# State-space convolution and FFN on one core: constants in another form and partly on GpSimd, another order around the first and last block

## The chip, the core and the metric

One core of one Trainium2 chip. The metric is the time of one execution in microseconds (us), for which before and after are compared by the median of several runs. The engines are TensorE (PE; PEld is its loading of weights), VectorE (DVE), ScalarE (ACT), GpSimd (POOL) and SyncE (SP, which here only issues DMAs).

## The reference

```python
# x: (128, 32, 512) f32, length: (128,)
K = 2 * Re(sum_n Ct[h,n] * exp(dtA[h,n] * l))            # (32, 512), Ct = C (exp(dtA) - 1) / A
y = causal_conv(x, K, over l) + x * D                     # channel by channel
y = y * (l < length[b])
x_q = fp8(y / in_scale); gate, up = x_q @ Wg.T, x_q @ Wu.T   # 512 -> 1376
hidden = silu(gate) * up
out = x + fp8(hidden / in_scale) @ Wd.T                   # 1376 -> 512
```

A is complex, with a real part -exp(log_A_real) and an imaginary part A_imag, and dtA = A dt. Rounding to fp8 is done in f32 arithmetic (a sum with a magnitude, a difference, a clip), the matmuls in bf16.

## The kernel before

The 32 channels are done in 8 blocks of 4, each with 4 x 128 = 512 tokens. A channel's convolution is one product of a Toeplitz matrix, cut from K with its D added at lag 0, with the transposed x: four f32 matmuls of 512, 384, 128 and 256 columns (L489). A block then has 11 chunks of the hidden width (c = 0 to 10, `slots`). For each, PE makes gate and up (L547, 4 + 4 matmuls of 512 columns), ACT the silu (L398), DVE the product `hv` (L860). Two chunks make a pair e = 0 to 5. For each pair ACT takes the magnitude `hc` (L381), DVE adds (`ht`, L868), rounds (`hq`, L877) and clips (L885), and `hq` is the operand of the down matmuls (L503), which PE does one block later, 4 a chunk. A convolution's result is masked (L825), scaled and rounded in the same way (L362 to L373 on ACT; `yt` L833, `yq` L844, L851 on DVE), one block ahead; the convolutions run up to two blocks ahead (CONV_PLAN).

The order is written out by hand on every engine. The tables at the end of the file (MASK_PLAN, SUM_PLAN, ROUND_PLAN, H_BEHIND, H_EVEN, H_LAST, OUT_SLOTS) say in which chunk a step of DVE or ACT stands. Chunk c of gate and up writes bank c mod 2 (with the block's parity) and so waits for the product of chunk c - 2 (L537). Pairs 3, 4 and 5 of a block are finished in the next one (`left_over`). The last block has no convolutions, and its own down matmuls stand behind it (L588 to L601), with the residual added by DVE (L892) and stored in five parts (LAST_PARTS).

Ahead of the blocks K has to be made. The parameters come in, DVE computes dt and A dt (to L686), from there exp(dtA) - 1 and C times it over A (L712 to L776), and with cos, sin and exp of the steps (`waves`, `decayed`) the operands `gk` of K (`g_of`, L788 to L792). This goes in three groups of channels: 4, 8 and 20 (K_GROUPS counts pairs). PE multiplies (`k_of`, L450, L454), the rows are copied out of PSUM (L802), SP stores them in DRAM (L241) and reads them back as Toeplitz matrices (L248, L252). Between, PE runs matmuls whose results are not used (`warm`, L471 and L459; WARM says how many). GpSimd issues the weight loads: `wg` and `wu`, the first 256 columns at once (L288, L289), the rest after the Toeplitz matrices.

## Time and profile before

| | us |
|---|---|
| median of 3 runs (325.57 to 326.49) | 325.71 |
| the profiled execution's own time | 325.52 |
| its span, first to last instruction | 323.8 |
| PE busy in it | 310.2 |
| DVE busy | 303.2 |
| ACT busy | 206.9 |

1.7 us of the profiled execution's time lie outside the span. The rows read below are from three views: the timeline (instructions of an engine in order of time, equal ones merged with their count), the waits, and the DMA issues. "x4" of an f32 matmul is two instructions, as each leaves two records; some records are missing ("x3" for four). A matmul's end is modelled: four of 512 columns are given as 1.03 us, while the next one starts 0.86 us after the first of them.

### The profile page before, as it was taken

How to read it: one execution, taken by the hardware profiler on the slowest of the kernel's cores; microseconds unless marked ns; L12 is line 12 of the kernel's file. 1: busy time of each engine (PE TensorE's matmuls, PEld its weight loads, DVE VectorE, ACT ScalarE, POOL GpSimd, SP SyncE). 2: the span in 40 equal slices, each digit the busy share in tenths (PEclk: the TensorE clock that was granted, in tenths of full speed). 3: DMA queues.
4: the chain of work that ended last, by engine and by line, in shares of the span. 5: the costliest groups of instructions: out<-in, count | busy, mean ns of one | idle time of the engine just before them, and what ended most of it. 6: DMA issues, size and time to landing. Idle time of an engine off the chain costs nothing.

```text
span 323.8 us, 4771 instructions
## 1 busy us (share of the span) xinstructions
PE 310.2 (96%) x1569; PEld 162.9 (50%) x1595; DVE 303.2 (94%) x464; ACT 206.9 (64%) x318; POOL 12.5 (4%) x20
## 2 busy tenths in 40 slices
PE   1999999999999999999999999999999999989996
PEld 1467554545455554555455454555455454534444
DVE  6999999999999999999998999989998999989784
ACT  4858788188755777486845868376863959364540
POOL 2031000000001000010001000010001000010010
PEclk9999999999999999999999999999999999999999
DMA  6879999300002690078202780067401650051028
GB/s 201 181 181 231 268 278 383 148 1 2 0 0 28 150 343 3 1 130 279 110 0 36 165 317 1 0 121 249 150 0 16 134 243 0 0 97 34 2 31 228
DMA packets 14014, 38.38 MB, mean 119 GB/s; under 512 B 1470, under 2 KB 6558, under 8 KB 11052
## 3 DMA queue, kind: packets, MB, share of 16 engines
q1 hardware_dynamic: 8412, 26.58, 23.2%
q0 software_dynamic: 5584, 11.57, 20.6%
q8 instruction: 10, 0.16, 0.2%
q14 instruction: 8, 0.07, 0.1%
HBM read 33.90 MB, written 15.81 MB: 154 GB/s over the span
## 4 chain that ended last, share of the span: by engine, by line
PE 72%; DVE 19%; issue 4%; ACT 4%; DMA 1%; DVEq 0%; ACTq 0%
PE gate_ps L547 19%; PE up_ps L547 18%; PE down_ps L503 17%; PE y_ps L489 15%; DVE hv L860 3%; DVE yq L844 3%; DVE yt L833 2%; DVE hq L877 2%; DVE ht L868 2%; PE y_ps L598 1%; DVE ym L825 1%; PE down_ps L598 1%; ACT hc L381 1%; DMA prm<-in_params 1%; DVE hq L885 1%
## 5 line engine op out<-in xcount | busy, mean ns | idle before, releaser
L398 ACT ACTIVATE sil<-gate_ps,fac 128x512 f32<-128x512 f32 (+1 forms) x88 | 59.6, 680 | 67.8 <-PE gate_ps L547 66.8
L547 PE MATMUL gate_ps<-yq,wg 128*128 128x512 bf16 (+3 forms) x365 | 88.2, 363 | 2.7 <-DVE hv L860 2.4
L547 PE MATMUL up_ps<-yq,wu 128*128 128x512 bf16 (+3 forms) x367 | 88.4, 363 | 0.3
L489 PE MATMUL y_ps<-xt,toep 128*128 128x512 f32 (+1 forms) x248 | 78.1, 434 | 0.0
L503 PE MATMUL down_ps<-wd,hq 128*128 128x512 bf16 (+1 forms) x295 | 76.8, 379 | 0.7
L860 DVE SCALAR_TENSOR_TENSOR hv<-up_ps,fac,sil 128x512 f32<-128x512 f32 (+1 forms) x88 | 65.5, 744 | 8.2 <-ACT sil L398 6.6
L381 ACT ACTIVATE hc<-hv 128x1024 f32<-128x1024 f32 (+1 forms) x48 | 47.0, 980 | 20.9 <-DVE hq L877 19.8
L547 PEld LDWEIGHTS gate_ps<-yq,wg 128*128 128x128 bf16 x372 | 35.6, 100 | 43.6 <-ACT sil L398 4.0
L489 PEld LDWEIGHTS y_ps<-xt,toep 128*128 128x128 f32 x248 | 45.9, 190 | 19.9 <-issue 2.4
L868 DVE SCALAR_TENSOR_TENSOR ht<-hc,hv 128x1024 f32<-128x1024 f32 (+1 forms) x48 | 54.1, 1127 | 1.9 <-ACT hc L381 1.9
L547 PEld LDWEIGHTS up_ps<-yq,wu 128*128 128x128 bf16 x372 | 36.3, 100 | 38.3
L877 DVE SCALAR_TENSOR_TENSOR hq<-hc,ht 128x1024 bf16<-128x1024 f32 (+1 forms) x48 | 53.8, 1126 | 0.3
L503 PEld LDWEIGHTS down_ps<-wd,hq 128*128 128x128 bf16 (+1 forms) x308 | 30.1, 98 | 37.9 <-issue 12.6
L844 DVE SCALAR_TENSOR_TENSOR yq<-yc,yt 128x1024 bf16<-128x1024 f32 x32 | 39.0, 1217 | 0.1
L833 DVE SCALAR_TENSOR_TENSOR yt<-yc,yv 128x1024 f32<-128x1024 f32 x31 | 37.7, 1217 | 0.0
L370 ACT ACTIVATE yc<-ym,fac 128x512 f32<-128x512 f32 x32 | 22.8, 713 | 2.9 <-DVE yq L844 2.9
L362 ACT ACTIVATE yv<-ym,fac 128x512 f32<-128x512 f32 x31 | 22.1, 712 | 3.2 <-DVE ym L825 3.2
L373 ACT ACTIVATE yc<-ym,fac 128x512 f32<-128x512 f32 x32 | 22.8, 712 | 0.0
L363 ACT ACTIVATE yv<-ym,fac 128x512 f32<-128x512 f32 x31 | 22.0, 709 | 0.0
L825 DVE TENSOR_TENSOR ym<-y_ps,mask 128x512 f32<-128x512 f32 x31 | 21.1, 681 | 0.0
L388 ACT ACTIVATE res<-down_ps,fac 128x512 f32<-128x512 f32 x28 | 19.0, 679 | 2.2 <-PE down_ps L503 2.1
L885 DVE TENSOR_SCALAR hq<-hq 128x1024 bf16<-128x1024 bf16 (+1 forms) x48 | 18.4, 397 | 0.3
(155 smaller groups left out, 118.1 us busy)
## 6 DMA issues: line engine op xcount, KB each, us to landing
xt<-in_xT SPq DMA_DIRECT2D x8, 1024.0 KB, 7.6
out<-in_x SPq DMA_DIRECT2D x7, 1024.0 KB, 5.6
out<-res POOLq DMA_DIRECT2D x7, 1024.0 KB, 7.8
toep<-kpad_scratch SPq DMA_DIRECT2D x6, 1024.0 KB, 10.0
toep<-kpad_scratch SPq DMA_DIRECT2D x8, 256.0 KB, 3.9
wd<-in_down POOLq DMA_DIRECT2D x1, 1280.0 KB, 21.3
xt<-in_x SPq DMA_DIRECT2D x1, 1024.0 KB, 7.3
out<-xt SPq DMA_DIRECT2D x3, 256.0 KB, 3.1
```

Source lines behind the costliest of these rows:

```text
L370: gate = nc.scalar.activation(yc[q][:, 0, :], ym[q][:], ACT.Abs, scale=fac[:, R_GATE:R_GATE + 1])
L381: nc.scalar.activation(hc[e % 2][0:w, 0:k], hv[e % 2][0:w, 0:k], ACT.Abs, scale=UP20).then_inc(abs_ready, 1)
L398: nc.scalar.activation(sil[b][0:w, :], gate_ps[b][0:w, :], ACT.Silu, scale=fac[0:w, S_GATE:S_GATE + 1]).then_inc(silu_done, 1)
L489: last = nc.tensor.matmul(y_ps[h % 2][:, d * P:L], toep[par][:, h, d * P:(d + 1) * P], xt[par][:, h, 0:L - d * P], start=(d == 0), stop=(d ...
L503: mm = nc.tensor.matmul(down_ps[t % 2][:], hq[par][0:w, k, t * P:(t + 1) * P], wd[0:w, k, :], start=(k == 0), stop=(k == CH - 1))
L547: mm = nc.tensor.matmul(ps[b][0:w, cols], wt[:, k, c * P:c * P + w], yq[par][:, version, k, cols], start=(k == 0), stop=(k == LB - 1))
L825: v.tensor_tensor(ym[q][:], y_ps[q][:], mask[:].rearrange("p k b -> p (k b)"), ALU.mult).then_inc(ym_done, 1)
L833: v.scalar_tensor_tensor(yt[q][:], yc[q][:], FLOOR, yv[q][:], ALU.max, ALU.add).then_inc(yt_done, 1)
L844: v.scalar_tensor_tensor(yq_of(par, h), yc[q][:].rearrange("p v (k b) -> p (v k) b", k=LB), FLOOR, yt[q][:].rearrange("p v (k b) -> p (v k ...
L860: v.scalar_tensor_tensor(hv[c // 2 % 2][0:w, c % 2], up_ps[b][0:w, :], fac[0:w, S_UP:S_UP + 1], sil[b][0:w, :], ALU.mult, ALU.mult).then_i ...
L868: v.scalar_tensor_tensor(ht[e % 2][0:w, 0:k], hc[e % 2][0:w, 0:k], FLOOR, hv[e % 2][0:w, 0:k], ALU.max, ALU.add).then_inc(t_done, 1)
L877: v.scalar_tensor_tensor(hq[par][0:w, 2 * e:2 * e + k, :], hc[e % 2][0:w, 0:k], FLOOR, ht[e % 2][0:w, 0:k], ALU.max, ALU.subtract, reverse ...
```

## The change

It has five parts. (1) The constants. With E = exp(Re dtA) - 1, h = 2 C / A and Q = h (exp(i Im dtA) - 1), the coefficient 2 Ct is (E + 1) Q + E h. The square of A's magnitude and the numerator of h come from five small products, sums and differences on GpSimd (L299 to L305 of the new file), behind a wait for `decay_ready` and ahead of its wait for the Toeplitz matrices. The D term of the first group is put into its bank ahead of time (`unit_terms(0)`, an operand 64 columns wider in `in_unit`). The lengths' masks move behind work for the second group. (2) WARM: one f32 matmul of 213 columns ahead of `k_of(0)` and one behind, 8 of 512 columns ahead of `k_of(1)` and 2 behind, for 2 and 14. (3) `hv` has three buffers. (4) Order: the fourth `yt` sum of each block is in chunk 9 for 8. At the boundaries 0 to 1 and 6 to 7 (SUM_BEHIND) the clip of pair 2 and the magnitude and sum of pair 4 come behind the first product of the next block; in block 7 the rest is spread over one chunk more. ACT's loop over blocks 1 to 4 is written out. (5) In block 7 the down matmuls of block 6 use four banks (`y_ps` as well) and another order, 4, 8, 6, 6, 5, 4, 4, 3, 2, 2 and 0 a chunk for 4 each; the last part of the output is 128 columns for 256.

```diff
-WARM = (2, 14)
+WARM = (1, 1, 8, 2)
...
-        hv = [sb(f"hv{i}", [P, 2, TOK]) for i in range(2)]
+        hv = [sb(f"hv{i}", [P, 2, TOK]) for i in range(3)]
...
+        unit_tile = inside(hq[0], JC * M, 1, P + FIRST * KB)
+        one_by_one = unit_tile[:, :, 0:P]
+        dsk_first = unit_tile[:, 0, P:].rearrange("p (j b) -> p j b", b=KB)
...
+            pool.wait_ge(decay_ready, 1)
+            nc.gpsimd.tensor_tensor(s(27), s(9), s(9), ALU.mult).then_inc(gain_chain, 1)
+            nc.gpsimd.tensor_tensor(s(31, 2), s(37, 2), s(9).broadcast_to([P, 2, JC]), ALU.mult).then_inc(gain_chain, 1)
+            pool.wait_ge(gain_chain, 1)
+            nc.gpsimd.tensor_tensor(s(27), s(27), s(28), ALU.add).then_inc(norm_ready, 1)
+            pool.wait_ge(gain_chain, 2)
+            nc.gpsimd.tensor_tensor(s(33), s(31), s(30), ALU.subtract)
+            nc.gpsimd.tensor_tensor(s(34), s(29), s(32), ALU.add).then_inc(gain_ready, 1)
...
-                nc.scalar.activation(hc[e % 2][0:w, 0:k], hv[e % 2][0:w, 0:k], ACT.Abs, scale=UP20).then_inc(abs_ready, 1)
+                nc.scalar.activation(hc[e % 2][0:w, 0:k], hv[e % 3][0:w, 0:k], ACT.Abs, scale=UP20).then_inc(abs_ready, 1)
...
+                from_bank = y_ps[t % 2] if isinstance(g, int) and g == NBLK - 2 and t >= 2 else down_ps[t % 2]
+                nc.scalar.activation(res[par][:, t, :], from_bank[:], ACT.Copy,
...
+                    if c == 0 and g - 1 in SUM_BEHIND:
+                        abs_prod(PAIRS * g - 2, PAIRS - 2, n - 1)
+                    if c and c % 2 == 0 and not (c == CH - 1 and g in SUM_BEHIND):
...
-            with act.Fori(0, (NBLK - 4) // 2) as j:
+            for j in range((NBLK - 4) // 2):
...
+                    if i == 0:
+                        nc.tensor.matmul(k_in_bank(0, half), unit_row, dsk_first[row], start=True, stop=False)
+                    else:
+                        nc.tensor.matmul(k_in_bank(i, half)[:, :, 0], unit_row, dsk[row, js],
+                                         start=False, stop=True).then_inc(k_ready, 1)
...
-                            nc.tensor.matmul(k_in_bank(i, half)[:, j - js.start], gk[rows, j, t],
-                                             wave[rows, j, t, 0:KB], start=(j == js.start and t == 0), stop=False)
-                for half in range(2):
-                    row = slice(N * half, N * half + 1)
-                    nc.tensor.matmul(k_in_bank(i, half)[:, :, 0], cst[row, UNIT:UNIT + KA], dsk[row, js],
-                                     start=False, stop=True).then_inc(k_ready, 1)
+                            last = i == 0 and j == js.stop - 1 and t == 1
+                            mm = nc.tensor.matmul(k_in_bank(i, half)[:, j - js.start], gk[rows, j, t],
+                                                  wave[rows, j, t, 0:KB], start=(i > 0 and j == js.start and t == 0),
+                                                  stop=last)
+                            if last:
+                                mm.then_inc(k_ready, 1)
+                if i:
+                    unit_terms(i)
...
-            for n in range(WARM[0]):
-                nc.tensor.matmul(y_ps[n % 2][:, 0:6 * JC + CONSTS], prm[:, 0:P], prm[:], start=True, stop=True)
+            unit_terms(0)
+            warm_small(WARM[0])
             k_of(0)
+            warm_small(WARM[1])
             pe.wait_ge(gate_in, 16)
-            warm(WARM[1])
+            warm(WARM[2])
             k_of(1)
+            warm(WARM[3])
...
+            def wide_down_part(g, par, c):
+
+                lo = sum(WIDE_COUNTS[:c])
+                for t, k in WIDE_ORDER[lo:lo + WIDE_COUNTS[c]]:
+                    w = width(k)
+                    if t == 0:
+                        pe.wait_ge(hq_ready, PAIRS * g + k // 2 + 1)
+                    if k == 0 and t < 2:
+                        pe.wait_ge(out_done, EMPTY + HB * g + t - 1)
+                    if k == 0 and t >= 2:
+                        pe.wait_ge(ym_done, HB * NBLK)
+                    mm = nc.tensor.matmul((y_ps if t >= 2 else down_ps)[t % 2][:], hq[par][0:w, k, t * P:(t + 1) * P],
+                                          wd[0:w, k, :], start=(k == 0), stop=(k == CH - 1))
+                    if k == CH - 1:
+                        mm.then_inc(down_ready, 1)
...
+                if down and not ahead:
+                    wide_down_part(g - 1, 1 - par, c)
+                elif down:
...
-                                    (2, range(6, CH), full), (3, range(CH), slice(0, L // 2)),
-                                    (3, range(CH), slice(L // 2, L))):
+                                    (2, range(6, CH), full), (3, range(CH), slice(0, 3 * P)),
+                                    (3, range(CH), slice(3 * P, L))):
...
-                    if t >= 2 and k == 0:
-                        pe.wait_ge(out_done, EMPTY + HB * (NBLK - 1) + t - 3)
+                    if k == 0:
+                        pe.wait_ge(out_done, EMPTY + HB * (NBLK - 2) + t + 1)
...
-            c = did(v.scalar_tensor_tensor(norm, ar, 0.5, ar, ALU.mult, ALU.mult))
+            v.tensor_scalar(two_x.bitcast(I32), kx, 127.0, 2.0 ** 23, ALU.add, ALU.mult)
+            dve.wait_ge(norm_ready, 1)
+            c = did(v.reciprocal(norm, norm))
             after(b)
             b = did(v.scalar_tensor_tensor(qx, qx, 1.0 / math.factorial(4), rx, ALU.add, ALU.mult))
-            v.tensor_tensor(c_ar, cc, both(ar), ALU.mult)
             after(b)
             b = did(v.scalar_tensor_tensor(qx, qx, 1.0 / math.factorial(3), rx, ALU.add, ALU.mult))
-            c = did(v.tensor_tensor(norm, norm, half, ALU.add))
+            v.tensor_tensor(rt_x, rx, two_x, ALU.mult)
+            dve.wait_ge(gain_ready, 1)
+            after(c)
+            c = did(v.tensor_tensor(h, h, both(norm), ALU.mult))
             after(b)
             b = did(v.scalar_tensor_tensor(qx, qx, 1.0 / math.factorial(2), rx, ALU.add, ALU.mult))
-            v.tensor_scalar(two_x.bitcast(I32), kx, 127.0, 2.0 ** 23, ALU.add, ALU.mult)
-            after(b)
-            b = did(v.scalar_tensor_tensor(qx, qx, 1.0, rx, ALU.add, ALU.mult))
-            c = did(v.reciprocal(norm, norm))
-            after(b)
-            b = did(v.tensor_tensor(qx, qx, two_x, ALU.mult))
-            v.tensor_tensor(gre, s(30), s(31), ALU.subtract)
-            c = did(v.tensor_tensor(gim, s(29), s(32), ALU.add))
+            dve.wait_ge(sines_ready, 1)
+            a = did(v.scalar_tensor_tensor(cos1, s(SIN_HALF), -2.0, s(SIN_HALF), ALU.mult, ALU.mult))
+            after(b)
+            b = did(v.scalar_tensor_tensor(qx, qx, 1.0, rt_x, ALU.add, ALU.mult))
             after(c)
+            c = did(v.tensor_tensor(h_sin, h, both(s(SIN)), ALU.mult))
+            after(a)
+            a = did(v.tensor_tensor(h_cos, h, both(cos1), ALU.mult))
+            after(b)
             b = did(v.scalar_tensor_tensor(expm1, two_x, -1.0, qx, ALU.add, ALU.add))
-            dve.wait_ge(sines_ready, 1)
-            a = did(v.scalar_tensor_tensor(sr, s(SIN_HALF), -2.0, s(SIN_HALF), ALU.mult, ALU.mult))
-            c = did(v.tensor_tensor(g, g, both(norm), ALU.mult))
             after(a)
-            a = did(v.scalar_tensor_tensor(sr, expm1, 1.0, sr, ALU.add, ALU.mult))
-            b = did(v.scalar_tensor_tensor(si, expm1, 1.0, s(SIN), ALU.add, ALU.mult))
+            v.tensor_tensor(s(35), s(29), s(32), ALU.subtract)
+            a = did(v.tensor_tensor(s(36), s(31), s(30), ALU.add))
             damped = [decayed(0)]
+            after(b)
             after(a)
-            a = did(v.tensor_tensor(sr, sr, expm1, ALU.add))
-            after(b)
-            b = did(v.tensor_tensor(g_si, g, both(si), ALU.mult))
+            v.scalar_tensor_tensor(h_cos, both(expm1), 1.0, turned, ALU.add, ALU.mult)
+            a = did(v.tensor_tensor(h_sin, both(expm1), h, ALU.mult))
             after(a)
-            a = did(v.tensor_tensor(g_sr, g, both(sr), ALU.mult))
-            after(a)
-            v.tensor_tensor(s(38), s(29), s(32), ALU.add)
-            a = did(v.tensor_tensor(s(39), s(31), s(30), ALU.subtract))
+            a = did(v.tensor_tensor(s(38, 2), h_cos, h_sin, ALU.add))
...
-            after(last)
-            v.tensor_scalar(mask[:, 0, :], lenf[:], cst[:, LEN0:LEN0 + 1], None, ALU.is_gt)
             after(w)
             v.tensor_tensor(turns[:, js], turns[:, js], whole[:, js], ALU.subtract).then_inc(turns_ready, 1)
             js = K_GROUPS[2]
             w = did(v.tensor_tensor(in_steps(turns[:, js]), tau_by_j(js), steps(js), ALU.mult))
+            after(last)
+            v.tensor_scalar(mask[:, 0, :], lenf[:], cst[:, LEN0:LEN0 + 1], None, ALU.is_gt)
+            after(w)
+            w = did(v.tensor_scalar(whole[:, js], turns[:, js], MAGIC, MAGIC, ALU.add, ALU.subtract))
             v.tensor_scalar(mask[:, 1, :], lenf[:], cst[:, LEN0 + 1:LEN0 + 2], None, ALU.is_gt)
             after(w)
-            w = did(v.tensor_scalar(whole[:, js], turns[:, js], MAGIC, MAGIC, ALU.add, ALU.subtract))
+            v.tensor_tensor(turns[:, js], turns[:, js], whole[:, js], ALU.subtract).then_inc(turns_ready, 1)
+            damped.append(decayed(1))
+            g_of(1)
             v.tensor_scalar(mask[:, 2, :], lenf[:], cst[:, LEN0 + 2:LEN0 + 3], None, ALU.is_gt)
-            after(w)
-            v.tensor_tensor(turns[:, js], turns[:, js], whole[:, js], ALU.subtract).then_inc(turns_ready, 1)
             v.tensor_scalar(mask[:, 3, :], lenf[:], cst[:, LEN0 + 3:LEN0 + 4], None, ALU.is_gt).then_inc(scales_ready, 1)
-            g_of(1)
+            damped.append(decayed(2))
...
+                    at_least(dve, t_done, m - 2)
+                v.scalar_tensor_tensor(hv[c // 2 % 3][0:w, c % 2], up_ps[b][0:w, :], fac[0:w, S_UP:S_UP + 1],
...
-            def left_over(g, par, c, before):
+            def left_over(g, par, c, before, behind):
 
                 last = PAIRS * g - 1
                 if c == 0:
                     if PAIRS - 3 not in before.values():
                         rounded(last - 2, g - 1, 1 - par, PAIRS - 3)
-                    rounded(last - 1, g - 1, 1 - par, PAIRS - 2)
+                    if not behind:
+                        rounded(last - 1, g - 1, 1 - par, PAIRS - 2)
                 if c == 1:
                     clip(last - 2, 1 - par, PAIRS - 3)
+                    if behind:
+                        rounded(last - 1, g - 1, 1 - par, PAIRS - 2)
+                    else:
+                        clip(last - 1, 1 - par, PAIRS - 2)
+                    rounded_sum(last, PAIRS - 1)
+                    if not behind:
+                        rounded(last, g - 1, 1 - par, PAIRS - 1)
+                        clip(last, 1 - par, PAIRS - 1)
+                if c == 2 and behind:
                     clip(last - 1, 1 - par, PAIRS - 2)
-                    rounded_sum(last, PAIRS - 1)
                     rounded(last, g - 1, 1 - par, PAIRS - 1)
                     clip(last, 1 - par, PAIRS - 1)
...
+                    if c == 0 and g - 1 in SUM_BEHIND:
+                        clip(PAIRS * g - 4, 1 - par, PAIRS - 4)
+                        rounded_sum(PAIRS * g - 2, PAIRS - 2)
...
-                        if PAIRS - 3 not in plan.values():
-                            clip(PAIRS * g + PAIRS - 4, par, PAIRS - 4)
-                        rounded_sum(m - 1, PAIRS - 2)
+                        if g not in SUM_BEHIND:
+                            if PAIRS - 3 not in plan.values():
+                                clip(PAIRS * g + PAIRS - 4, par, PAIRS - 4)
+                            rounded_sum(m - 1, PAIRS - 2)
...
-SUM_PLAN = {2: 0, 3: 1, 6: 2, 8: 3}
...
+SUM_PLAN = {2: 0, 3: 1, 6: 2, 9: 3}
...
+SUM_BEHIND = (0, NBLK - 2)
...
+WIDE_ORDER = [(t, k) for chunks in (range(6), range(6, CH)) for t in range(HB) for k in chunks]
+WIDE_COUNTS = [4, 8, 6, 6, 5, 4, 4, 3, 2, 2, 0]
...
-              (HB - 1, 0, slice(0, L // 2)), (HB - 1, 1, slice(L // 2, L))]
+              (HB - 1, 0, slice(0, 3 * P)), (HB - 1, 1, slice(3 * P, L))]
```

The diff is cut to what the text speaks of; left out are the operand of the D term, the bank of each tile at the end (now `down_ps`, `down_ps`, `y_ps`, `y_ps`), and the products with -2 C at the start of DVE's chain, one instruction more.

The first place is VectorE while the constants of the kernel K are computed, from the turns of the first two channels to the copy of their K out of PSUM. `sm` holds all small operands. Before:

```order
L751 TENSOR_SCALAR sm<-sm 128x16
L753 SCALAR_TENSOR_TENSOR sm<-sm 128x16 [waits chain]
L754 RECIPROCAL sm<-sm 128x16
L756 TENSOR_TENSOR sm<-sm 128x16 [waits chain]
L757 TENSOR_TENSOR sm<-sm 128x16
L758 TENSOR_TENSOR sm<-sm 128x16
L760 SCALAR_TENSOR_TENSOR sm<-sm 128x16 [waits chain]
L762 SCALAR_TENSOR_TENSOR sm<-sm 128x16 [waits sines_ready]
```

The same place now, with two waits for GpSimd:

```order
L799 TENSOR_SCALAR sm<-sm 128x16
L801 RECIPROCAL sm<-sm 128x16 [waits norm_ready]
L803 SCALAR_TENSOR_TENSOR sm<-sm 128x16 [waits chain]
L805 SCALAR_TENSOR_TENSOR sm<-sm 128x16 [waits chain]
L806 TENSOR_TENSOR sm<-sm 128x16
L809 TENSOR_TENSOR sm<-sm 128x32 [waits chain,gain_ready]
L811 SCALAR_TENSOR_TENSOR sm<-sm 128x16 [waits chain]
L813 SCALAR_TENSOR_TENSOR sm<-sm 128x16 [waits sines_ready]
```

Between line 741 and the first product with `wave` (L788 before, L843 now) stood 24 instructions and stand 19 now. Five others are on GpSimd, between its early weight loads and the next. The row L299 ISA is an instruction that the builder puts ahead of the first arithmetic on this engine; its name in the built program is a reload of the engine's code library, index 0. GpSimd now:

```order
L293 DMA wu<-in_up 128x4x256
L299 ISA
L299 TENSOR_TENSOR sm<-sm 128x16 [waits decay_ready]
L300 TENSOR_TENSOR sm<-sm 128x32
L302 TENSOR_TENSOR sm<-sm 128x16 [waits gain_chain]
L304 TENSOR_TENSOR sm<-sm 128x16 [waits gain_chain]
L305 TENSOR_TENSOR sm<-sm 128x16
L307 DMA wg<-in_gate 128x4x384 [waits toep_first3]
```

Before, L289 was followed by L291 (now L307) directly.

The second place is VectorE at the boundary from block 6 to block 7 (`hv` is a product, `ht` the sum that rounds it, `hq` the rounded operand of the down matmuls). Before:

```order
L860 SCALAR_TENSOR_TENSOR hv<-up_ps,fac,sil 96x512 [waits t_done,up_ready,silu_done]
L877 SCALAR_TENSOR_TENSOR hq<-hc,ht 128x1024 [waits t_done]
L885 TENSOR_SCALAR hq<-hq 128x1024 [waits hr_done]
L868 SCALAR_TENSOR_TENSOR ht<-hc,hv 128x1024 [waits hr_done,abs_ready]
L860 SCALAR_TENSOR_TENSOR hv<-up_ps,fac,sil 128x512 [waits t_done,up_ready,silu_done]
L877 SCALAR_TENSOR_TENSOR hq<-hc,ht 128x1024 [waits t_done] x2
```

Now:

```order
L917 SCALAR_TENSOR_TENSOR hv<-up_ps,fac,sil 96x512 [waits t_done,up_ready,silu_done]
L934 SCALAR_TENSOR_TENSOR hq<-hc,ht 128x1024 [waits t_done]
L917 SCALAR_TENSOR_TENSOR hv<-up_ps,fac,sil 128x512 [waits t_done,up_ready,silu_done]
L942 TENSOR_SCALAR hq<-hq 128x1024 [waits hr_done]
L925 SCALAR_TENSOR_TENSOR ht<-hc,hv 128x1024 [waits hr_done,abs_ready]
L934 SCALAR_TENSOR_TENSOR hq<-hc,ht 128x1024 [waits t_done]
L917 SCALAR_TENSOR_TENSOR hv<-up_ps,fac,sil 128x512 [waits up_ready,silu_done]
```

The first product of block 7 now stands ahead of the clip and the sum that finish block 6, and the second ahead of one rounding more. The boundary from block 0 to 1 has the same exchange, with both roundings ahead of the second product.


## Rows read from the trace of the kernel before

**Rows 1.** The page, part 1: busy time and share of the span of each engine

```profile
PE 310.2 (96%) x1569; PEld 162.9 (50%) x1595; DVE 303.2 (94%) x464; ACT 206.9 (64%) x318; POOL 12.5 (4%) x20
```

**Rows 2.** Waits of PE: waited for, us in total, times, longest

```profile
PE gate_ps L547 <- DVE hv L860: 2.4, 5, 1.0
```

**Rows 3.** Timeline of PE before the first block: start us, us, instruction, [idle before]

```profile
12.40 4.57 PE L459 MATMUL y_ps<-wg 128*128 128x512 bf16 x14
16.90 0.64 PE L450 MATMUL gate_ps<-res,hq 64*16 64x32 f32 x32
17.77 0.92 PE L560 MATMUL y_ps<-xt,toep 128*128 128x256 f32 x4
```

**Rows 4.** Timeline of VectorE (DVE) in the same stretch

```profile
8.09 0.17 DVE L741 SCALAR_TENSOR_TENSOR sm<-sm 128x16 f32<-128x16 f32 x1
...
10.97 0.23 DVE L788 TENSOR_TENSOR hq<-res,sm 128x64 f32<-128x64 f32 x1
...
12.50 0.34 DVE L802 COPY hq<-down_ps 16x64 f32<-16x64 f32 x2 [0.27 <-PE down_ps L454]
12.78 0.27 DVE L804 TENSOR_SCALAR mask<-lenf,prm 128x128 f32<-128x128 f32 x1
```

**Rows 5.** DMA issues of SyncE, and the landing of those of line 248

```profile
12.87 0.36 SPq L241 DMA_DIRECT2D kpad_scratch<-hq  x1
14.36 1.75 SPq L248 DMA_DIRECT2D toep<-kpad_scratch  x4
```

```profile
DMA to landing us min/median/max: 3.4/3.7/4.0
```

**Rows 6.** Timeline of GpSimd (POOL) before the first block, then early DMAs to landing

```profile
0.88 0.19 POOL L284 MEMSET zrow<- 32x128 f32 x1 [0.29 <-POOLq L1072]
3.96 0.93 POOL L288 DMA_DIRECT2D wg<-in_gate  x1 [2.89 <-DMA kpad_scratch<-zrow]
4.88 0.77 POOL L289 DMA_DIRECT2D wu<-in_up  x1
```

```profile
wg<-in_gate POOLq DMA_DIRECT2D x1, 256.0 KB, 8.4
```

**Rows 7.** Timeline of ScalarE (ACT): a load of its function table

```profile
7.05 1.28 ACT L328 ACT_TABLE_LOAD   x1
```

**Rows 8.** Block 0 to block 1: PE, then DVE

```profile
61.43 0.82 PE L547 MATMUL gate_ps<-yq,wg 128*128 128x384 bf16 x4 [0.60 <-DVE hv L860]
```

```profile
60.45 0.74 DVE L860 SCALAR_TENSOR_TENSOR hv<-up_ps,fac,sil 128x512 f32<-128x512 f32 x1
...
65.09 0.41 DVE L885 TENSOR_SCALAR hq<-hq 128x1024 bf16<-128x1024 bf16 x1
65.76 1.23 DVE L868 SCALAR_TENSOR_TENSOR ht<-hc,hv 128x1024 f32<-128x1024 f32 x1 [0.26 <-ACT hc L381]
67.13 0.75 DVE L860 SCALAR_TENSOR_TENSOR hv<-up_ps,fac,sil 128x512 f32<-128x512 f32 x1
```

**Rows 9.** Block 6 to block 7: timeline of PE

```profile
285.15 1.03 PE L503 MATMUL down_ps<-wd,hq 128*128 128x512 bf16 x4
287.19 1.02 PE L547 MATMUL gate_ps<-yq,wg 128*128 128x512 bf16 x4 [1.01 <-DVE hv L860]
288.05 1.03 PE L547 MATMUL up_ps<-yq,wu 128*128 128x512 bf16 x4
...
297.40 1.26 PE L503 MATMUL down_ps<-wd,hq 128*128 128x512 bf16 x4
```

**Rows 10.** The end: PE, then DVE

```profile
309.73 1.03 PE L547 MATMUL up_ps<-yq,wu 128*96 128x512 bf16 x4
```

```profile
310.86 0.75 DVE L860 SCALAR_TENSOR_TENSOR hv<-up_ps,fac,sil 96x512 f32<-96x512 f32 x1 [0.69 <-ACT sil L398]
...
315.91 0.29 DVE L885 TENSOR_SCALAR hq<-hq 96x512 bf16<-96x512 bf16 x1
...
321.21 0.48 DVE L892 SCALAR_TENSOR_TENSOR xt<-gate_ps,fac,xt 128x256 f32<-128x256 f32 x1 [0.72 <-PE gate_ps L598]
```

53 lines of the change are left out of this document (31 added, 22 removed).

## The prediction

> **What bounds the kernel now.** I read the page first: PE is busy for 310.2 us of 323.8 and DVE for 303.2 [rows 1]. Two engines are nearly full, so a step is worth what the engine that is late at that place gains. Of PE's waits, those of gate matmuls for a product of DVE are 2.4 us in five places [rows 2]. The timeline puts them at 37.9 us (block 0 begins), at 61.4 (block 0 to 1) and at 287 to 293 (6 to 7). In between PE has no idle time, and blocks repeat every 37.15 us. The chunks around the first and the last blocks hold more DVE work than PE work, since PE has no down matmuls in block 0 and no or few convolutions in 6 and 7.
>
> Ahead of the blocks the end is set by a chain: constants on DVE (L741 at 8.09, operands at 10.97), rows of K, their copy at 12.50 [rows 4], their store at 12.87 and the Toeplitz loads at 14.36, of which the first lands 3.4 us later, at 17.7 [rows 5], and the first convolution at 17.77 [rows 3]. From there PE runs without a gap to 35. The matmuls of the warm-up (14 in 4.57 us from 12.40, where 14 at 0.216 would take 3.0) begin at 0.43 us each, the lower clock (1.2 GHz), and end at 0.216, the higher one (2.4 GHz) [rows 3]; in their starts the change lies at 15.3 us.
>
> **The chain to the first convolution.** Between 8.09 and 10.97, 24 instructions stand, 0.12 us each [rows 4]; five fewer give 0.6 us. One more at the start of DVE's chain costs 0.05. The two D matmuls of the first group, 0.14 us ahead of the copy at 12.50, go to before the constants are ready, where PE has a gap. So the copy comes at 11.8, 0.7 us earlier, the store at 12.2, and by the same 1.5 and 3.4 us the first Toeplitz matrix at 17.0. The store now meets the end of the early weight loads; the bound for that is 0.3 us of the 0.7.
>
> The second group must be through PE by then. DVE's operands for it were ready at 16.85 (PE began on them at 16.90 [rows 3]). They come 0.7 us earlier by the copy, and about 0.4 more since two masks (0.27 us long, pitch 0.2 [rows 4]) are now behind them: 15.8. PE, with one small warm-up (0.9 us) after the first group, starts the eight large ones at 12.6, six of them at 0.43 and the last at 0.216 if the clock rises where it did: 15.7. The second group takes 0.8, to 16.6, two further matmuls 0.43, to 17.05. The convolution starts at 17.1 to 17.3: I take **-0.6 us** (bounds -0.3 and -0.75). DVE's first mask, at 19.57 before, has the whole 0.7 us and doesn't hold this up.
>
> What GpSimd does has to be in time. It is free at 5.65 (4.88 + 0.77 [rows 6]), the norm is wanted at 8.26 and the gain at 8.72 (8.09 plus the pitches ahead). No row shows arithmetic on GpSimd. Its memset of 32x128 took 0.19 us [rows 6]; five of that are 0.95, from 6.1 to 7.05. The upper end is a DMA issue's 0.93 each, 4.65: gain at 10.7, 2.0 late. The nearest in kind is the memset, so 0. Ahead of them stands the reload of its code library, which no row shows either. Below, the nearest row is ACT's load of its function table, 1.28 us [rows 7]: 5.65 + 1.28 + 0.95 is 7.9, in time. Above it is a transfer in the same stretch: the 256 KB of `wg`, issued at 3.96, took 8.4 us to land [rows 6]. Up to 2.1 us are hidden. I take the table load, since it is the same kind of step, and keep the transfer as a rival.
>
> The Trainium skill (GPSIMD Engine Reference, section 4.1) puts two-input elementwise work on GpSimd at about half VectorE's speed. By DVE's 0.17 us for such tiles that would be 5 x 0.34, ready at 7.8 without the reload: the same conclusion as from the memset.
>
> **Block 0 to 1.** PE sat idle 0.60 us for the product of chunk 9 at 60.45 [rows 8]. With the `yt` sum (1.13 us of pitch) behind it, that product is at 59.3 and PE's gap goes. Next comes DVE's own gap: from the clip at 65.09 to the first product of block 1 at 67.13 there are 2.04 us for 0.34 + 1.14 of work, as DVE waits for ACT's magnitude (0.26) and then for the semaphore [rows 8]. The product is now first, silu is ready by 64.2, and the 0.56 us go. DVE has no further idle time until 84.7 us, where PE once more waits 0.2 us for a product, so PE gets what DVE gains: **-0.55 us** (bounds 0, and -0.9 with all that PE loses there).
>
> **Block 6 to 7.** Three waits for products, 1.01, 0.18 and 0.22, plus 0.16 each, because an end is modelled 0.16 us late (the matmuls at 285.15 are through at 286.02, the next start at 287.19 [rows 9]): 1.9 us. At 297.40 four down matmuls took 1.10 us to the next start instead of 0.86, waiting for ACT to empty a bank [rows 9]: 0.23. With four banks that goes. In the new order the first product of block 7 is at 284.0 (silu of the last part of chunk 0 ends then) instead of 286.29, the second at 287.4 instead of 289.2. PE, with 4 and 8 down matmuls in chunks 0 and 1, asks for them at 286.9 and 289.9. Going on like this to chunk 10, I find each product at least 1 us early. The clip of pair 2 ends as PE comes to its matmuls (both 285.1), 0 to 0.1 us. So PE gains 2.1 us and ends the last up matmul at 309.36 instead of 311.46.
>
> Some of it is given back. Before, the last up matmuls ended at 310.59, DVE took the product at 310.86 and had the last clip at 316.20, 5.34 us later [rows 10]; PE wanted it at 316.65. Now no down matmul stands behind the last up matmuls: product at 309.63, last clip at 314.97, wanted 24 matmuls after 309.36, at 314.55. With 0.05 for the semaphore that is a new wait of 0.5. Sum **-1.6 us** (bounds -0.9 and -2.1).
>
> **The tail.** Both halves of the last tile stay at 11 x 512 columns together. The last residual of 256 columns took 0.48 us [rows 10]; for 128 it is about 0.13 less, and its store is smaller: **-0.1** (0 to -0.2). The third `hv` buffer takes away waits that show none of PE's idle time: 0 by itself, but it lets products go ahead of sums. ACT's written-out loop: 0, it is idle 1 to 3 us in each block.
>
> **Sum.** -0.6 - 0.55 - 1.6 - 0.1 = -2.85 against the profiled execution's 325.52: 322.67. The median is 0.19 above that execution, so 322.8. By the bounds alone: 321.7 to 324.5. A measurement of this kernel can tell about 0.3% (1 us) from no change.
>
> **Rivals.** (a) *The reload costs what a transfer costs.* With 8.4 us it ends at 14.05, the gain is ready at 15.0, and DVE, which waits for it in order at 8.72, has everything behind it 6.3 us later: the rows of K, all masks, the first convolution. PE idles from 10.5 on. The blocks' gains stay, so the time is 322.8 + 6.3 = 329.1; if PE then starts its convolutions at the lower clock, up to 1.5 more. The reload decides from 2.1 us on, and at 5.0 us (2.1 + 2.9) the change is worth nothing. For it: code has to come from somewhere, and DMA is full from 5 us on. Against: ACT's load of the same sort is 1.28 us beside the same traffic.
>
> (b) *The two engines hold each other up.* Five GpSimd instructions of 0.19 us that each stop DVE once give 0.95 us: 323.7. The Trainium skill (SBUF, section on who interferes with whom) says that a VectorE instruction with two SBUF inputs and a GpSimd one that reads SBUF lock each other out; most of DVE's instructions between 6.1 and 8.7 are such, and no row here has both at work.
>
> (c) *The clock is not up when the convolutions start.* PE has less work before 15.3 us than before. Eight warm-ups at 0.43 end at 16.0, two at 0.43 end at 17.9 with the group, and the first channel takes 4.4 us for 2.2: 322.8 + 0.6 + 2.2 = 325.6, no change.
>
> **How the numbers follow.** Forecast 0.50, (a) 0.36, (b) 0.07, (c) 0.07. The likeliest case gives 322.8, its own range 321.7 to 324.5. The range reaches from 321.9 to 330.6 to hold most of (a) too. Faster is the forecast, (b) and some of (c): 0.58. Same: the rest of (c) and a reload of about 5 us, 0.06. Slower: 0.36.
>
> **What would show it.** In the new profile: GpSimd's first arithmetic at about 7 us, DVE's reciprocal (L801) without idle time before it, operands of K at 10.4, the copy at 11.8, the first convolution at 17.2; no idle time of PE at 61 and 287, and one of 0.4 us before the last down matmuls of tile 0. Wrong: GpSimd's products at 13 us or later with DVE idle until then (a); DVE instructions of 16 columns that take 0.3 (b); 512-column matmuls of 0.43 us after 16 us (c). If PE still idles at 287, my order of products is wrong.

## The result and the profile after

Over 7 runs each, the changed kernel takes 323.43 us (323.10 to 324.86) and the one before 325.82 (325.57 to 326.76): a ratio of 0.9933, with a 95% interval of 0.992 to 0.9945. That is 2.4 us less in this comparison; over the later comparisons the kernel before stays at 325.6 and the difference is 2.1.

The changed kernel has two profiles. The first, of its slowest run (324.86 us, span 323.2), has one disturbed stretch, told below. The second is of the same kernel (the first experiment, 323.38 us, span 321.7) and is typical; rows are of this one unless the text says otherwise. The table puts them beside [rows 3, 8, 9, 10].

| start, us | before | after, 2nd profile | after, 1st profile |
|---|---|---|---|
| first convolution | 17.77 | 17.63 | 19.14 |
| gate matmuls of chunk 7, block 1 | 84.70 | 84.17 | 85.64 |
| gate matmuls of block 7 | 280.81 | 280.29 | 281.77 |
| first of the last down matmuls | 311.46 | 308.94 | 310.42 |
| span | 323.8 | 321.7 | 323.2 |

GpSimd, as the timeline of the first profile has it (start us, us, instruction), answers to [rows 6]:

```profile
5.04 0.76 POOL L293 DMA_DIRECT2D wu<-in_up  x1
6.09 0.21 POOL L299 TENSOR_TENSOR sm<-sm 128x16 f32<-128x16 f32 x1 [0.29 <-DVE sm L743]
6.27 0.25 POOL L300 TENSOR_TENSOR sm<-sm 128x32 f32<-128x32 f32 x1
...
6.86 0.26 POOL L305 TENSOR_TENSOR sm<-sm 128x16 f32<-128x16 f32 x1
```

The five operations take 0.21 to 0.26 us each, 0.2 apart, and are through at 7.12; no reload of a library is seen ahead of them. Nor is one hidden behind the wait for VectorE: in the profile of the run with both mended (the last but two below) GpSimd's last early DMA issue ends at 6.03 and its first operation starts at 6.12, without idle time. By the Trainium skill (GPSIMD Engine Reference, section 4.1), at half VectorE's speed, the estimate was 0.34 each and 7.8; they are quicker than that.

VectorE in the second profile [rows 4]:

```profile
8.12 0.17 DVE L798 SCALAR_TENSOR_TENSOR sm<-sm 128x16 f32<-128x16 f32 x1
8.20 0.17 DVE L799 TENSOR_SCALAR sm<-sm 128x16 int32<-128x16 f32 x1
8.28 0.25 DVE L801 RECIPROCAL sm<-sm 128x16 f32<-128x16 f32 x1
...
10.48 0.22 DVE L843 TENSOR_TENSOR hq<-res,sm 128x64 f32<-128x64 f32 x1
...
11.87 0.34 DVE L857 COPY hq<-down_ps 16x64 f32<-16x64 f32 x2
```

VectorE waits for nothing at L801. The step that began at 8.09 before begins at 8.12, K's operands come 0.49 us earlier and the copy 0.63 earlier. PE and SyncE [rows 3, 5]:

```profile
12.64 3.56 PE L496 MATMUL y_ps<-wg 128*128 128x512 bf16 x8
16.13 0.64 PE L482 MATMUL gate_ps<-res,hq 64*16 64x32 f32 x32
...
16.84 0.61 PE L496 MATMUL y_ps<-wg 128*128 128x512 bf16 x2
17.63 0.92 PE L617 MATMUL y_ps<-xt,toep 128*128 128x256 f32 x4 [0.18 <-DMA toep<-kpad_scratch]
```

```profile
12.24 0.36 SPq L245 DMA_DIRECT2D kpad_scratch<-hq  x1
14.18 1.75 SPq L252 DMA_DIRECT2D toep<-kpad_scratch  x4
```

The store leaves 0.63 us earlier than before, but the Toeplitz loads that wait for it leave only 0.18 earlier: it takes 1.94 us now and took 1.49 before. PE is ready for the convolution and waits for the load.

In the first profile the same store and loads stand at 12.22 and 14.34, but the loads landed after 4.8 us at the soonest, where before they took 3.4 [rows 5]. A table by stretches (width, busy times by engine, PEclk, DMA share, GB/s) shows the DMA engines occupied and moving next to nothing:

```profile
15.00:15.50 0.50, 0.26 (x2) 0.00 (x0) 0.47 (x3) 0.50 (x2) 0.00 (x0) 1.00 0.99 29
15.50:16.00 0.50, 0.18 (x12) 0.18 (x14) 0.50 (x4) 0.50 (x1) 0.00 (x0) 1.00 1.03 29
```

No other profile here has it. From the first convolution on the two profiles of the changed kernel keep 1.5 us apart to the end.

### The profile page after: what moved, and what is told of

Same layout as the page of the kernel before. It is cut to its first block, busy times and chain, and to the rows that moved or that the text cites. A ratio compares the mean times of both kernels' runs of the same rounds, so it can differ in the third digit from the quotient of the medians.

```text
span 323.2 us, 4716 instructions
## 1 busy us (share of the span) xinstructions
PE 310.3 (96%) x1591; PEld 161.8 (50%) x1591; DVE 303.1 (94%) x460; ACT 206.5 (64%) x318; POOL 13.7 (4%) x25
## 4 chain that ended last, share of the span: by engine, by line
PE 77%; DVE 15%; issue 3%; DMA 3%; ACT 2%; DVEq 0%; SPq 0%
PE gate_ps L604 20%; PE up_ps L604 20%; PE down_ps L542 17%; PE y_ps L528 15%; DVE hv L917 3%; DVE yq L901 2%; DVE ht L925 2%; DVE yt L890 2%; DVE hq L934 2%; PE down_ps L558 2%; PE y_ps L558 1%; DMA toep<-kpad_scratch 1%; DVE ym L882 1%; PE y_ps L655 1%; DMA kpad_scratch<-hq 1%
## 5 line engine op out<-in xcount | busy, mean ns | idle before, releaser
L604 PE MATMUL gate_ps<-yq,wg 128*128 128x512 bf16 (+2 forms) x372 | 89.5, 363 | 0.5 <-DVE hv L917 0.3
L604 PE MATMUL up_ps<-yq,wu 128*128 128x512 bf16 (+2 forms) x372 | 89.5, 363 | 0.0
L542 PE MATMUL down_ps<-wd,hq 128*128 128x512 bf16 (+1 forms) x264 | 67.9, 379 | 0.0
L397 ACT ACTIVATE hc<-hv 128x1024 f32<-128x1024 f32 (+1 forms) x48 | 47.0, 980 | 17.1 <-DVE hq L934 16.7
L542 PEld LDWEIGHTS down_ps<-wd,hq 128*128 128x128 bf16 (+1 forms) x264 | 25.8, 98 | 32.7 <-issue 12.0
L942 DVE TENSOR_SCALAR hq<-hq 128x1024 bf16<-128x1024 bf16 (+1 forms) x48 | 18.5, 396 | 0.3
L405 ACT ACTIVATE res<-down_ps,fac 128x512 f32<-128x512 f32 x26 | 17.6, 677 | 1.0 <-PE down_ps L542 1.0
```

Of the source, the lines that this page charges most:

```text
L397: nc.scalar.activation(hc[e % 2][0:w, 0:k], hv[e % 3][0:w, 0:k], ACT.Abs, scale=UP20).then_inc(abs_ready, 1)
L542: mm = nc.tensor.matmul(down_ps[t % 2][:], hq[par][0:w, k, t * P:(t + 1) * P], wd[0:w, k, :], start=(k == 0), stop=(k == CH - 1))
L604: mm = nc.tensor.matmul(ps[b][0:w, cols], wt[:, k, c * P:c * P + w], yq[par][:, version, k, cols], start=(k == 0), stop=(k == LB - 1))
```

## Experiments

Times are medians; before is 325.6 us in all three comparisons (325.63, 325.58 and 325.67). Each kernel's median is over 5 to 12 runs. A ratio in brackets is to the kernel before, followed by its 95% interval.

**The changed kernel again.**

> The changed kernel once more, unaltered. My sum (prologue -0.6, block 0 to 1 -0.5, block 7 -1.6, tail -0.1) put it at 322.8 us; its median was 323.4, and in the one profile of it the transfers of K came in 1.4 to 2 us later than before. If that lateness was chance, this profile has the first convolution at 17.1 to 17.5 us and the Toeplitz loads landing 3.4 to 4.0 us after issue. If it belongs to the change (the earlier store meets the end of the weight loads every time), the convolution starts at 18.5 to 19.1 again and the loads take 4.8 us or more. Median 323.1 to 323.8 in either case.

Measured: 323.53 us (0.9932, interval 0.9918 to 0.9946). The convolution is at 17.63 and the four loads take 3.4 to 4.1 us, 3.8 in the middle: neither the 17.1 to 17.5 of the one theory nor the 18.5 of the other. The slow loads of the first profile were chance (one of 14 profiles has them, and their cause stays open); the slow *store* is not, as the next runs show.

**The start alone, and the blocks alone.** The first part of the change on the kernel before, and parts two to five on it.

> The kernel before with the first part of the change alone (complex product, five operations on GpSimd, D matmuls first, warm-ups 1, 1, 8, 2), the blocks as before. By my sum -0.6 us (325.2). By the rival that the transfers of K eat the earlier store: 0, between -0.2 and +0.2, or later than before where the loads take 4.8 us, up to +1.3.

> The kernel before with the rest of the change (third product buffer, order at blocks 0 to 1 and 6 to 7, four banks, last part of 128 columns), the start as before. By my sum -2.25 us (323.5 to 323.6), PE without idle time at 61 and 287, a wait of 0.5 ahead of the last down matmuls of tile 0. If the prologue gives nothing, this one has the time of the whole change (323.4). If the blocks had brought less than I put down and the prologue its 0.6, it would be at 324.0.

Measured: the start alone 325.41 us (0.999, 0.998 to 1.0), the blocks alone 323.75 (0.9941, 0.9927 to 0.9954). That is 0.22 and 1.88 us less, 2.10 together, which is the whole change. The start alone can't be told from nothing by its time; by its profile the convolution begins at 17.56 after a store of 2.0 us (issued at 12.31, loads at 14.30). With the blocks alone the start is row for row as before: convolution at 17.77, store 1.48 us.

The profile of the blocks alone prices each place in a clean way. Block 0 to 1, two rows of PE before that [rows 8] does not have, then PE and DVE with the blocks alone:

```profile
71.55 1.02 PE L547 MATMUL gate_ps<-yq,wg 128*128 128x512 bf16 x4
...
280.81 0.82 PE L547 MATMUL gate_ps<-yq,wg 128*128 128x384 bf16 x4
```

```profile
60.72 0.81 PE L568 MATMUL gate_ps<-yq,wg 128*128 128x384 bf16 x4
...
71.14 1.02 PE L568 MATMUL gate_ps<-yq,wg 128*128 128x512 bf16 x4 [0.26 <-DVE hv L881]
```

```profile
59.36 0.74 DVE L881 SCALAR_TENSOR_TENSOR hv<-up_ps,fac,sil 128x512 f32<-128x512 f32 x1
60.02 1.22 DVE L854 SCALAR_TENSOR_TENSOR yt<-yc,yv 128x1024 f32<-128x1024 f32 x1
61.27 1.23 DVE L865 SCALAR_TENSOR_TENSOR yq<-yc,yt 128x1024 bf16<-128x1024 f32 x1
...
65.26 0.73 DVE L881 SCALAR_TENSOR_TENSOR hv<-up_ps,fac,sil 128x512 f32<-128x512 f32 x1
```

PE's wait at 61 is gone (61.43 to 60.72) and half of it comes back at 71, where PE waits for DVE: 71.55 to 71.14, and at block 7 280.81 to 280.46. So this place gives 0.35 us (0.40 if counted from the first gate matmuls of 512 columns, which were at 37.98 for 37.93 already). DVE closed its gap of 0.56 but lost 0.11 on the way: its `yt` sum and the rounding that reads it now stand side by side, and the second begins 1.25 us after the first, where two independent ones of this size are 1.14 apart. The other 0.05 up to the 0.40 that its products gain (70.66 to 70.26) it was late before: its sum at 57.84 is at 57.89 here.

Block 7 [rows 9, 10], first the row of before at which its own last down matmuls begin:

```profile
311.46 3.62 PE L598 MATMUL y_ps<-wd,hq 128*128 128x512 bf16 x16
```

```profile
280.46 0.81 PE L568 MATMUL gate_ps<-yq,wg 128*128 128x384 bf16 x4
...
284.91 1.90 PE L522 MATMUL down_ps<-wd,hq 128*128 128x512 bf16 x8
286.65 1.03 PE L568 MATMUL gate_ps<-yq,wg 128*128 128x512 bf16 x4
...
309.12 3.62 PE L619 MATMUL down_ps<-wd,hq 128*128 128x512 bf16 x16
...
313.87 0.60 PE L619 MATMUL down_ps<-wd,hq 128*128 128x512 bf16 x2
314.77 1.04 PE L619 MATMUL down_ps<-wd,hq 96*128 96x512 bf16 x4 [0.31 <-DVE hq L906]
```

No wait for a product is left at 285 to 300; one of 0.11 for the clip of pair 2 stands ahead of the down matmuls at 284.91 (the up matmuls from 283.94 are through at 284.80). The last up matmuls are through at 309.12 instead of 311.46, of which 0.35 came with block 1: block 7 gives 1.99. The new wait for the last clip is there: two down matmuls of 0.216 are followed after 0.90, so 0.47.

**GpSimd's five operations back on VectorE.** Between the same steps of the two chains, for example:

```diff
-            dve.wait_ge(norm_ready, 1)
+            d = did(v.tensor_tensor(s(34), s(29), s(32), ALU.add))
+            after(c)
             c = did(v.reciprocal(norm, norm))
```

> The whole change, but the five operations of GpSimd put back on VectorE between the same steps of the two chains, where none waits for its forerunner. By my price of 0.12 us each the operands of K, their copy and the first convolution come 0.6 us later, and the time is up by 0.6, if K's transfers take the same. If the transfers absorb what the start gains (they end when the early weight loads are through), the time is up by 0 to 0.2, and the Toeplitz loads land at the same time as in the change.

Measured: 323.69 us (0.9936, 0.9923 to 0.9948), 0.16 more than the change, which is within the spread of the single runs. The copy is at 12.28 (0.41 later than 11.87) and the store at 12.65; this transfer takes 1.76, so the loads leave at 14.41 and the convolution starts at 17.79. Of 0.41 us in the chain 0.16 reach the convolution: K's transfers absorb the rest, most of it in the store (1.76 for 1.94), as the second theory says; that they end when the early weight loads are through is not shown by this run. Moving five operations to GpSimd is worth 0.41 in the chain (0.08 each, not my 0.12) and 0.16 at the convolution.

**Less traffic in front of K's store.**

```diff
             load_x_t(0, 0)
-            load_x_t(1, 1)
...
                 sp.dma_start(toep[0][:, h], toep_d[0, :, h]).then_inc(toep_first[h], 16)
+            load_x_t(1, 1)
             store_k(1)
```

> The whole change, but the load of the second block's x (1 MB, issued at the start, ahead of all that the prologue waits for) is issued behind the first four Toeplitz loads. So far K's store was issued at 12.3 to 12.9 and landed at 14.2 to 14.4 in every profile. If it lands only when the early loads are through, then with 1 MB less at some 400 GB/s (2.5 us) these end at about 11, the store at 12.24 takes the 1.4 us of the kernel before and lands at 13.7, the first convolution is at 17.1 and the time is 0.5 less (323.0). If the store's landing has another cause (a fixed latency, its own order), nothing moves in it and the time is 323.5. Against both: the moved 1 MB now runs beside the Toeplitz loads; if these slow down by it, the convolution is at 18 to 19 and the time up by 0.5 to 1.5.

Measured: 325.71 us (0.9996, 0.9978 to 1.0015), so the gain of the change is lost. The twelve runs fall in two groups: six at 324.2 to 325.3 with a mean granted clock of 1.000, six at 326.1 to 327.1 with 0.994 or 0.995; the profile is of one of the second group. Yet the store does what the first theory says. Issued at 12.24, it lets the loads leave at 13.71, and PE starts the convolution at 17.00:

```profile
17.00 0.82 PE L617 MATMUL y_ps<-xt,toep 128*128 128x256 f32 x4
...
31.19 4.11 PE L528 MATMUL y_ps<-xt,toep 128*128 128x512 f32 x8 [2.96 <-DMA toep<-kpad_scratch]
```

DMA share and GB/s while the store was under way, in the change and here:

```profile
12.50:13.00 0.50, 0.50 (x2) 0.20 (x2) 0.50 (x2) 0.49 (x3) 0.00 (x0) 1.00 0.96 138
13.00:13.50 0.50, 0.50 (x3) 0.15 (x2) 0.50 (x4) 0.50 (x3) 0.00 (x0) 1.00 0.41 52
```

```profile
12.50:13.00 0.50, 0.50 (x2) 0.15 (x1) 0.50 (x2) 0.49 (x3) 0.00 (x0) 1.00 0.00 0
13.00:13.50 0.50, 0.50 (x3) 0.16 (x2) 0.50 (x4) 0.50 (x3) 0.00 (x0) 1.00 0.12 17
```

So K's 8 KB take 1.47 us where nothing else is in flight and 1.94 where loads still are. The Trainium skill (DMA: Bandwidth & Descriptors, section on latency and other measured facts) has the fixed cost of a transfer smaller when memory is lightly loaded, which agrees. A doubt that the traffic is the whole cause comes from the run with x in halves, below. What I had not counted: the 1 MB now runs beside the *second* store of K, which takes 6.9 us to land (1.7 before, 2.4 in the change), so the Toeplitz loads of block 1 leave at 24.04 instead of 19.80. And PE, idle for 2.96 us until they land, goes on at the lower clock (the third number from the end is PEclk, in parts of 2.4 GHz):

```profile
31.00:33.00 2.00, 1.81 (x3) 0.97 (x4) 0.19 (x1) 0.22 (x1) 0.00 (x0) 0.67 1.11 271
33.00:35.00 2.00, 2.00 (x6) 1.25 (x5) 0.00 (x0) 0.00 (x0) 0.00 (x0) 0.50 1.14 278
```

The next eight records of convolutions take 4.11 us for 2.38: another 1.7 us for the same wait. This is the second group's price; the first group lost 0.7 us or more without it.

**Six matmuls into PE's last wait.** The first down matmuls of tile 3 go ahead of the last ones of tiles 0 and 1:

```diff
-                                    (2, range(6), full), (0, range(8, CH), full), (1, range(8, CH), full),
-                                    (2, range(6, CH), full), (3, range(CH), slice(0, 3 * P)),
+                                    (2, range(6), full), (3, range(6), slice(0, 3 * P)), (0, range(8, CH), full),
+                                    (1, range(8, CH), full), (2, range(6, CH), full), (3, range(6, CH), slice(0, 3 * P)),
```

> The whole change, but in the end the first six down matmuls of tile 3 (384 columns) go ahead of the last ones of tiles 0 and 1. They fill PE's wait for the last clip (0.45 us: starts at 313.69 and 314.59 for two matmuls of 0.216). If that wait is what the shorter block 7 gave back, PE has no idle time there and the time is 0.45 less. If the last residuals and stores set the end, it stays.

Measured: 323.33 us (0.9929, 0.9916 to 0.9942), 0.1 to 0.2 less than the change's 323.43 and 323.53, not 0.45; so small a difference lies within the spread of the runs, and the profile has to tell. PE's wait is gone and its last group starts at 317.97 instead of 318.34, though this run began its block 7 0.10 later. But the span, counted from the start of block 7, is only 0.2 shorter (41.2 for 41.4 us). The stores take the rest. In stretches of 1 us, first the change, then this kernel:

```profile
319.00:320.00 1.00, 0.12 (x3) 0.00 (x0) 0.51 (x2) 0.00 (x0) 0.00 (x0) 1.00 0.88 338
```

```profile
319.00:320.00 1.00, 0.00 (x0) 0.00 (x0) 0.13 (x1) 0.00 (x0) 0.00 (x0) 1.00 1.04 396
```

Once PE is through, the DMA engines are full with the five stores of 1 MB in all, and the last of them, 64 KB, takes 2.0 us to land where it took 1.7.

**The old order at 6 to 7, and the old banks.** First VectorE's and ScalarE's order of before with four banks; then the new order with two banks and four down matmuls to a chunk.

```diff
-SUM_BEHIND = (0, NBLK - 2)
+SUM_BEHIND = (0,)
...
-                behind = g == NBLK - 1
+                behind = g - 1 in SUM_BEHIND and g > 1
```

```diff
-                if down and not ahead:
-                    wide_down_part(g - 1, 1 - par, c)
-                elif down:
+                if down:
                     down_part(g - 1, 1 - par, c)
```

> The whole change, but VectorE and ScalarE take the end of block 6 and the start of block 7 in the order of before; the down matmuls of block 6 stay 4, 8, 6, 6 ... to a chunk in four banks. By my sum the order was what brings PE's 1.9 us and the banks only 0.23 of it: then the time is up by 1.3 to 1.9. The rival: 8 down matmuls at a chunk cover a late product as well as an early product does, so each part alone is enough: up by 0.3 to 0.6, from the first product alone (286.3 + 0.7, where PE wants it at 286.5).

> The whole change, but the down matmuls of block 6 come four to a chunk in two banks again, and the last ones in the banks of before; VectorE's and ScalarE's new order stays. By my sum the order alone takes away 1.9 of PE's waits; the bank wait of 0.23 comes back, and with four down matmuls behind the last up ones there is no new wait at the end (0.5 less). Time: same to 0.3 less. The rival (the order alone is not enough, PE runs into VectorE in the chunks where it has no work to put in between): waits for products at 287 to 300, 0.5 to 1.5 us in sum, and the time up by as much less 0.5.

Measured: the old order 323.51 us (0.9933, 0.9921 to 0.9946), just the change's time; the old banks 324.76 (0.9972, 0.9963 to 0.9982), 1.2 more. My sum had it the other way round. With the old order, PE then DVE:

```profile
284.72 1.95 PE L558 MATMUL down_ps<-wd,hq 128*128 128x512 bf16 x8
286.65 1.02 PE L604 MATMUL gate_ps<-yq,wg 128*128 128x512 bf16 x4
```

```profile
285.76 0.75 DVE L917 SCALAR_TENSOR_TENSOR hv<-up_ps,fac,sil 128x512 f32<-128x512 f32 x1
```

The product is 2.1 us later than with the new order and through at 286.51, just as PE wants it: eight down matmuls of 0.216 keep PE busy to 286.45, and it goes on at 286.65. Of these 0.2 us 0.1 come back, since here the eight need not wait for the clip of pair 2. (I had put it at 286.3, its place before, and forgot the half microsecond that the earlier parts had already won.) With the old banks, PE then DVE:

```profile
291.98 0.61 PE L542 MATMUL down_ps<-wd,hq 128*128 128x512 bf16 x2 [1.36 <-DVE hq L940]
...
296.74 1.27 PE L542 MATMUL down_ps<-wd,hq 128*128 128x512 bf16 x4
```

```profile
291.50 0.42 DVE L940 TENSOR_SCALAR hq<-hq 128x1024 bf16<-128x1024 bf16 x1
```

No product is late now, but the clip of pair 4, which the new order put one product and one sum further back, is: PE, done with six chunks of tiles 0 and 1, wants it in chunk 3. In four banks the first 24 down matmuls need pairs 0 to 2 alone, and PE comes to the later clips well after them. That wait (1.36 and the modelled 0.16) and the old one for a bank (1.11 to the next start for 0.86) make up the 1.76 us that block 7 is longer; the wait at the end is gone, as expected.

From the first gate matmuls of block 7 (280.81 before) to the first of the last down matmuls (311.46) it is 30.65 us before, 30.41 with the new order alone, 28.72 with the four banks and their order alone, and 28.65 with both.

**x in halves, and both together.** Channels 0 and 1 of the second x at the start, the rest behind the eighth Toeplitz load; then also three matmuls of tile 3, `(3, range(3), slice(0, 3 * P))`, ahead.

```diff
-            load_x_t(1, 1)
+            sp.dma_start(xt[1][:, 0:2], xT[1, :, 0:2]).then_inc(xt_in[1], 16)
...
+            sp.dma_start(xt[1][:, 2:4], xT[1, :, 2:4]).then_inc(x_rest, 16)
             store_k(2)
```

> The whole change, but of the second block's x only channels 0 and 1 (0.5 MB) are loaded at the start, the rest behind the eighth Toeplitz load. With all of it moved the store landed after 1.4 us and the first convolution began at 17.0, but the later Toeplitz loads came too late. If the bytes in flight at 12.2 to 14 us are what holds the store, 0.5 MB less ends them at about 12.3, the store lands at 13.7 to 13.8, the first convolution is at 17.0 to 17.2 and, with the second half of x out of the way of the Toeplitz loads, PE keeps the 0.5 us to the end: 323.0. If the store's landing depends on something else about x, the convolution stays at 17.6. If the rest of x now delays block 1, PE waits for a DMA between 28 and 42 us, and the gain is lost.

> As the run before (x in halves), and three of the first down matmuls of tile 3 ahead of the last ones of tiles 0 and 1. With six of them PE's wait was gone and its last tile came 0.4 us earlier, but tiles 0 and 1 and their stores came 0.5 us later, and the time fell by 0.1 to 0.2. If the stores (4 x 256 KB) were what took it back, three matmuls (0.49 us) fill the wait of 0.5 without delaying them, and this gives 0.3 to 0.45 less than the run before; if PE's end doesn't set the time at all, 0.1 to 0.2 less.

Measured: 324.08 us (322.90 to 328.06; 0.9957, 0.9931 to 0.9982) and 323.19 (322.67 to 326.14; 0.9944, 0.9917 to 0.997). The lowest times are the lowest of all kernels here, the medians show no gain that can be told, and five runs are about 3 us longer or more. Four of these have a mean clock of 0.995 of the full one, as the run with all of x moved had in its profile; one (326.08) has 1.000. That the four lost the clock to the same kind of wait is likely and not shown, since none of them was profiled, and what the fifth lost its time to is open. In the two profiles the store took 1.83 us (issued at 12.26) and 1.48 (issued at 12.42), though the loads ahead of it ended at much the same time, with a DMA share of 0.11 and 0.04 from 12.5 to 13 us. So either a sixth of a microsecond in the issue decides, or the traffic is not all of it; this is open. The convolution began at 17.38 and 17.93. In the second it wasn't the load that PE waited for:

```profile
12.81 3.62 PE L498 MATMUL y_ps<-wg 128*128 128x512 bf16 x8
16.36 1.04 PE L484 MATMUL gate_ps<-res,hq 64*16 64x32 f32 x32
...
17.48 0.61 PE L498 MATMUL y_ps<-wg 128*128 128x512 bf16 x2
17.93 0.81 PE L621 MATMUL y_ps<-xt,toep 128*128 128x256 f32 x4
```

All eight warm-ups ran at the lower clock and so did the group of K (1.04 us for 0.64); the higher one came at about 17.3. PE reached the convolution 0.9 us after the 17.0 of the run with all of x moved. The three matmuls did fill the wait at the end: from the first gate matmuls of 512 columns (37.97, and 37.53 without them) the last group comes 0.48 us sooner, but the span ends only 0.14 sooner. That is the 0.1 to 0.2 that I had set down for the case that PE's end does not set the time.

**The `yt` sum back in chunk 8.** `SUM_PLAN = {2: 0, 3: 1, 6: 2, 8: 3}`, the order of products as in the change.

> The whole change, but VectorE makes the fourth yt sum in chunk 8 again, as before. By my sum PE gets at block 0 to 1 what VectorE gains, and that is its own idle time (0.56) closed by the product ahead of the sum; the place of the yt sum matters only for where PE waits: PE's gap at 61 us is back (0.3 to 0.6), but that of 0.26 at 71 goes, and at 84 us PE stands where it stood or 0.1 earlier, since the pair of dependent instructions (yt sum and its rounding, pitch 1.25 where 1.14 is usual) is apart again. Time: -0.15 to +0.05. The rival (the yt sum's place is what brings the gain): 0.2 to 0.6 more.

Measured: 323.65 us (0.9941, 0.9928 to 0.9954), 0.1 to 0.2 more than the change. PE's wait of 0.60 at 61 is back and that at 71 is gone, as I said, but chunk 7 of block 1 is at 84.43 instead of 84.17, with the first convolution at the same time: 0.26 later, not earlier. The reason is on ScalarE and DVE:

```profile
64.34 0.69 ACT L415 ACTIVATE sil<-gate_ps,fac 128x512 f32<-128x512 f32 x1 [4.63 <-PE gate_ps L604]
```

```profile
65.33 0.75 DVE L917 SCALAR_TENSOR_TENSOR hv<-up_ps,fac,sil 128x512 f32<-128x512 f32 x1 [0.28 <-ACT sil L415]
```

PE late at 61 makes silu late at 64.3, and DVE, whose gap the new order was to close, has a new one before the same product. The two edits need each other: of the 0.39 us that they bring in the change (0.53 at 84 us less the 0.14 of the start), 0.14 are the order's alone (84.70 to 84.43, less 0.13).

**No warm-ups.** `WARM = (0, 0, 0, 0)`: PE's twelve products that nothing reads are left out.

> The whole change, but with none of PE's twelve warm-up matmuls (their products go nowhere). It prices the clock: if they are what brings the 2.4 GHz clock up before the first convolution, the first convolution starts as before (it waits for the Toeplitz load) at 17.6, its matmuls of 256 and 512 columns take twice their time until the clock rises, PE is 1.5 to 2.5 us later in the blocks and the time is 1 to 2.5 more. If the clock rises in time by the matmuls of K alone, no difference.

Measured: 325.70 us (324.46 to 326.25; 0.9995, 0.9984 to 1.0007), 2.2 more than the change. The convolution starts at 17.75, at the lower clock, as the time of its matmuls shows (1.65 us for 0.92):

```profile
17.75 1.65 PE L617 MATMUL y_ps<-xt,toep 128*128 128x256 f32 x4 [0.55 <-DMA toep<-kpad_scratch]
```

## Why the prediction was right, and where it was not

The forecast was 322.8 us, by -2.85 against the profile of before; measured are 323.43 and, from profile to profile (325.52 to 323.38), -2.14. The terms below, as measured, add up to between -2.1 and -2.3. The likeliest case was the one that came, and each of the three rivals is out by a row.

| term | predicted | measured | from |
|---|---|---|---|
| chain to the first convolution | -0.6 | -0.14 to -0.21 | 17.63, and 17.56 with the start alone |
| block 0 to 1 | -0.55 | -0.35 to -0.40 | 280.46 for 280.81, blocks alone, which were 0.05 late at 37.9 |
| block 6 to 7, gained | -2.1 | -1.99 | 309.12 for 311.46, less the 0.35 |
| given back before the last clip | +0.5 | +0.47 | 314.77 after 313.87 |
| tail | -0.1 | -0.13 | last residual 0.35 us for 0.48; with the blocks alone the span is 2.0 less and PE's last group through at 319.30 for 321.17 |

**The chain.** The mis-sized step is "the store at 12.2, and by the same 1.5 and 3.4 us the first Toeplitz matrix at 17.0". Copy and store came as I put them (11.87 and 12.24 for 11.8 and 12.2). The 1.5 was not the same, since I took a duration from a row in which the store was issued as the traffic ended (12.87), and used it at 12.24, inside the traffic. I named this collision and bounded it by 0.3; it is 0.45. The run with x moved shows 1.47 once the traffic is gone, and a convolution at 17.00, as I had put it; there it starts as PE's last warm-up ends, without a wait for the load. Five operations fewer gave 0.52 us there (8.09 to 10.97 became 8.12 to 10.48), not 0.6.

**Block 0 to 1.** "PE gets what DVE gains" holds, but DVE gained 0.45 in this place and not 0.56: a rounding right behind the sum that it reads costs 0.11 more.

**Block 6 to 7.** The size was right and its reason wrong. I worked out the 1.9 from the earlier products and gave the banks 0.23; the 4 and 8 matmuls stood in my sum only as the time at which PE asks. The runs with one of the two undone show that the order adds 0.07 us to the banks with their 4 and 8 matmuls, which bring 1.93 of 2.00, and by itself brings 0.24. So the number came out by luck: with the order alone I would have forecast 1.9. My sign of an error, PE idle at 287, could not have caught this, since PE has no such wait with the old order either. "Going on like this to chunk 10, I find each product at least 1 us early" looked at products only; with two banks a clip, which the order delays, would have taken their place.

**The new wait** came as worked out from the old path of 5.34 us. Removing it gives PE 0.47 us and the span 0.1 to 0.2; the last stores, with the DMA engines full, take the rest.

**Rivals.** (a) The reload: GpSimd's first operation starts 0.29 us after its DMA issue, in one profile 0.09, and DVE never waits for it. (b) The lock between the engines: DVE's step at 8.09 is at 8.12, and the only rows between 6.1 and 7.15 that are longer by more than 0.01 us are L746 with 0.19 for 0.17 and L780 with 0.21 for 0.17. At most 0.03 us, so the rule of the Trainium skill (SBUF — State Buffer, section on who interferes with whom) costs next to nothing in this place. (c) The clock: it was up at the first convolution in all profiles with warm-ups, but at 16.1 us in the second profile and about 17.3 in another, where I had taken 15.3 as fixed. Without warm-ups the loss is 2.2 us, the size that I gave to a first channel at the lower clock.

**Not shown.** No run has the third `hv` buffer or ACT's written-out loop alone, so my 0 for each is untested, and the products ahead of the sums at block 0 to 1 were never undone by themselves.

## What to carry to other kernels

A duration of a small transfer holds for the traffic beside it: before moving a store earlier, look what the DMA engines do at its new time, and what a transfer moved out of its way will meet. Where PE waits for a product, matmuls of other work put ahead of it can help as much as an earlier product, as here, and don't delay anything else on VectorE; but they are missing where they were taken from, which is why the last clip is waited for now; after planning an order, check the producers that it puts *last* as well as those that it puts first. Before adding two edits up, ask whether each one's gain rests on the other's.

## What the runs showed of the hardware

- GpSimd: `tensor_tensor` of 128x16 and 128x32 f32 in 0.21 to 0.26 us, 0.2 apart, with its semaphores. VectorE's of this size are 0.17 to 0.19.
- A store of 8 KB that is read back took 1.47 to 1.49 us in the four profiles in which the loads were through or ending at its issue, and 1.76 to 2.12 in the ten others, where it was issued with loads in flight. One of 16 KB took 1.7 us before, 2.4 in the change and 6.9 beside 1 MB on the same queue.
- VectorE: two instructions of 1024 columns, the second reading the first's result, 1.25 us apart; independent ones 1.14.
- TensorE: after 2.96 us without work the granted clock was 0.50 (1.2 GHz) for most of the next 4 us. When it rises at the start differs between runs: eight warm-ups of 512 columns took from 2.41 to 3.62 us in eleven profiles. The Trainium skill (TensorE: Matmul & The Clock Gate, part 1, what's actually happening) says as much, that the count of slow matmuls varies from run to run of a kernel.
- PEclk in the tables stood at 1.00 also from 12 to 15 us, where matmuls of 512 columns took 0.43 us: at the start of a kernel it is their spacing that shows the clock.
